# A MetaFormer layer on one core: reordered side work, and the first expert product packed by rows

## The chip, the cores and the metric

The kernel runs on one core of a Trainium2 chip. The metric is the device time of one execution in microseconds. The kernel before took 605.97 us in the median of three runs (603.32 to 607.88).

## The reference

The input x has 4 images of 96 channels and 56 x 56 pixels in fp32. The layer has two halves.

1. **Super-token attention.** Each pixel is normalised over its channels. The image is cut into 7 x 7 cells of 8 x 8 pixels; the mean of a cell is a super token. Each pixel has a softmax over the 9 super tokens around it (the affinities). Weighted sums of pixels give new super tokens, which go through attention with 8 heads of 12 (softmax over 49 tokens) and a projection; the result is spread back to the pixels by the affinities and added to x.
2. **A mixture of experts.** Each pixel is normalised again. A gate picks 2 of 4 experts. Each expert is `gelu(t @ w1 + b1) @ w2 + b2` with w1 96 x 384 and w2 384 x 96; the sum, weighted by the gate, is added to x. The kernel computes all four experts for each pixel, with weight 0 for those not picked.

```
h = gelu(einsum('bsd,edh->ebsh', x, w1) + b1)
y = einsum('ebsh,ehd->ebsd', h, w2) + b2
out = einsum('bse,ebsd->bsd', masked, y)
```

## The kernel before

An image is 28 tiles of 112 pixels. Four tiles are a **unit** of 448 pixels (the 8 rows of one row of cells). For each unit and each expert there is a **slot**: 28 slots an image, 112 in all. Everything else of an image is **side work**, done for image b+1 or b+2 between the slots of image b. All queues are written out by hand, with semaphores; nothing is planned by a program. TABLE names, for slot and half of slot, which side step PE does; READER names the engine that reads the step's bank. BEFORE is the order ahead of the first slot, the head.

**A slot.** `first_layer(i)` (L1121) makes z for 384 hidden values in three banks. The operands are split in fp16 high and low parts, so each third takes three products of 448 columns: w1_hi with the tokens' high part, w1_hi with their low part, w1_lo with the high part; 97 rows each, 96 channels and one of ones that brings in the bias. Two sets of three banks alternate. ACT reads z twice, GELU to fp16 (`hidden_high`, L469) and GELU to fp32 (`hidden_full`, L477). DVE takes the difference (`low_part`, L811). `second_layer(i)` puts the bias in with one product of 384 columns (L1130), then 24 products of 96 columns with the high part (L1136) and 12 with the low part (L1141), into one bank, Y. DVE adds the bank to xt in four instructions, weighted by the gate (`add_expert`, L824). PE's order in slot i is: side step, first_layer(i+2), side step, second_layer(i). The first layer waits for h_ready of slot i-2, the second for sum_done of slot i-1. DVE's order is: side read, low_part(i+1), side read, further side work, add_expert(i).

**Side work by kind.** SF (L962): sums of cells, read by DVE; CEN: centring, read by ACT; LOG (L978): affinity logits and gate logits, read by DVE; affinity_shift on DVE, exp on ACT, sums and scales on DVE and POOL; SFT (L989): the super sums over 28 tiles, in four parts; SUPT, QKV, SCO, PRT, HEA, HET, PRO: the attention, in small products; AFT: turned affinities; PIX (L1065): pixels out of super tokens, added by DVE; TRN (L1076): turned tokens for the first layer, copied by ACT (L436) to xhl.

**Deviations.** The first normalisation's 1/sqrt (`deviation_begin`, `deviation_end`) and the second's (`pixel_variance`, `pixel_deviation`) are chains of small DVE instructions with a wait after each: a shift trick for the start and three Newton steps of three instructions, on 112 x 28 values.

**Tables.** ACT uses Exp for the affinities (slot 2), for the attention (slot 9) and for the gate (slot 23), and GELU in each slot. Each change loads a table.

**Queues.** SP has the input transfers, one transfer of b2's low part, the channel loads (`load_channels`, 1.2 MB each), and one store a unit. ACT's queue has the constants and the weights at the start.

The names that the change touches:

Of the kernel before, what the change touches and what calls it, by code (L numbers as in the profile page):

```python
# [50 lines left out]
NORMAL = {0: 2, 3: 3, 8: 4, 13: 5, 17: 6}  # L51
# [6 lines left out]
def constants():  # L58
# [16 lines left out]
    ones = np.tile(np.concatenate([np.ones(IMG), np.zeros(IMG)]), 2)[None]  # L75
    return (table.astype(np.float32), row.astype(np.float32), cells.astype(np.float32), near.astype(np.float32),
            ones.astype(np.float16))


def build(nc, x, xtok, table, inner, cells, near, ones, wqkv, wproj, bproj, projx, gate_w, gate_b, w1, b1, w2, b2, out):  # L80

    with ExitStack() as ctx:
# [18 lines left out]
        scrap = sb("scrap", [1, 2])  # L101
        spare = sb("spare", [1, 1])
# [6 lines left out]
        w1_hi = sb("w1_hi", [CB, E * HID], F16)  # L109
        w1_lo = sb("w1_lo", [CB, E * HID], F16)  # L110
# [20 lines left out]
        seed = sb("seed", [PT, T], I32)  # L131
# [14 lines left out]
        prob = sb("prob", [128, 4, N])  # L146
        probT = sb("probT", [N, 4, 128])
# [6 lines left out]
        xhl = sb("xhl", [CB, 2, 2, IMG], F16)  # L154
# [13 lines left out]
        def own_super(r0, r1):  # L168
# [4 lines left out]
        w1_st = stage[0:CB, 0:E * HID]  # L173
# [8 lines left out]
            ones_in zeros_set pool_set ident16_set gatew_done gatew_set w_hi weights_set  # L182
            cell_ready shifted exp_ready scale_ready aff_ready affr_ready
            aff_hi aff_lo prob_ready so_hi so_mid norm_ready xs_ready xhi_ready xlo_ready
            gate_shifted gate_exp gate_ready
            side_done side_act side_dve z_done hh_ready h_ready hl_ready y_done sum_done
            norm1_step norm2_step attn_step gate_step weights_step""".split()
# [13 lines left out]
                  + [(0, "PIX", 0), (1, "SF", 0), (0, "PIX", 1), (1, "SF", 1), (0, "PIX", 2), (1, "SF", 2),  # L201
                     (0, "PIX", 3), (1, "SF", 3), (0, "PIX", 4), (0, "PIX", 5), (0, "PIX", 6), (1, "CEN", 0)]
                  + [(1, "LOG", k) for k in range(4)] + [(0, "TRN", 0)])
        BETWEEN = [(0, "TRN", 1)]

        TABLE = {(2, 0): (0, "TRN", 2), (5, 0): (0, "TRN", 3),
                 (6, 0): (1, "SFT", 0, 0, 4), (6, 1): (1, "SFT", 0, 1, 4), (7, 0): (1, "SFT", 0, 2, 4),
                 (7, 1): (1, "SFT", 0, 3, 4), (8, 0): (1, "SUPT", 0), (8, 1): (1, "QKV", 0), (9, 0): (1, "SCO", 0),
                 (9, 1): (1, "AFT", 0), (10, 0): (1, "AFT", 1), (10, 1): (0, "TRN", 4), (11, 0): (1, "PRT", 0),
                 (11, 1): (1, "HEA", 0), (12, 0): (1, "HET", 0), (12, 1): (1, "PRO", 0), (13, 0): (1, "PRO", 1),  # L210
                 (13, 1): (1, "AFT", 2), (14, 0): (1, "AFT", 3),
                 (15, 0): (1, "PIX", 0), (15, 1): (2, "SF", 0), (16, 0): (1, "PIX", 1), (16, 1): (2, "SF", 1),
                 (17, 0): (1, "PIX", 2), (17, 1): (0, "TRN", 5), (18, 0): (1, "PIX", 3), (18, 1): (2, "SF", 2),
                 (19, 0): (1, "PIX", 4), (19, 1): (2, "SF", 3), (20, 0): (1, "PIX", 5), (20, 1): (2, "CEN", 0),
                 (21, 0): (1, "PIX", 6), (21, 1): (0, "TRN", 6), (22, 0): (2, "LOG", 0), (22, 1): (2, "LOG", 1),
                 (23, 0): (2, "LOG", 2), (23, 1): (2, "LOG", 3), (25, 0): (1, "TRN", 0), (27, 0): (1, "TRN", 1)}
# [16 lines left out]
        visits += [(v, SIDE) for v in BETWEEN]  # L233
# [23 lines left out]
        def last_before_slots(bank):  # L257

            return [u for u, where in visits[0:len(BEFORE)] if where == bank][-1]
# [9 lines left out]
        def project_rows(k):  # L269
            return (range(0, 5), range(5, G))[k]  # L270

        @block.sync
        def _(sp):
# [17 lines left out]
            sp.dma_start(b2_hl[1:2, :], b2_low[:]).then_inc(S["b2_moved"], 16)  # L291
            for b in range(B):
                if b + 2 < B:
                    sp.wait_ge(S["side_done"], number[(b + 1, "LOG", 3)] + 1)
                    load_channels(b + 2)
                for r in range(G):
                    sp.wait_ge(S["sum_done"], b * SLOTS + (r + 1) * E)
                    sp.dma_start(out[b * IMG + r * UT:b * IMG + (r + 1) * UT, :].rearrange("(t p) c -> p t c", p=PT),
                                 rows_of(b, r)[:, :, 0:C]).then_inc(S["out_stored"], 16)
# [3 lines left out]
        def _(pool):  # L303
            for n, (what, value) in enumerate((
                    (ones16[:], 1.0), (aoT[:], 0.0), (vT[:], 1.0), (qm[:], 0.0), (gw[:], 0.0),
                    (hh[:, :, :, UT:FW], 0.0), (hl[:, :, :, UT:FW], 0.0), (aff16[:], 0.0))):
                pool.memset(what, value).then_inc(S["pool_set"], 1)
                pool.wait_ge(S["pool_set"], n + 1)
# [13 lines left out]
            def tokens_low(b, r):  # L322
# [3 lines left out]
                pool.tensor_tensor(x16[:, rows, 1, :], xs[:, rows, :], x16[:, rows, 0, :], ALU.subtract  # L326
                                   ).then_inc(S["xlo_ready"], 1)

            affinities_low(0)
            for r in range(2):  # L330
                tokens_low(0, r)
            for b in range(B):
                for slot in range(SLOTS):
                    if slot in NORMAL:
                        tokens_low(b, NORMAL[slot])
                    if b + 1 < B:
                        if slot == 4:
# [3 lines left out]
                        if slot in (23, 24):  # L341
                            tokens_low(b + 1, slot - 23)

        @block.scalar
        def _(act):
            for dst, src, name in (
# [3 lines left out]
                    (wqkv_sb[:], wqkv, "small_in"), (gate_bb[:], gate_b.to_broadcast([128, E]), "small_in"),  # L350
                    (xhl[C:CB, :, :, :].rearrange("p i h n -> p (i h n)"), ones, "ones_in")):
                act.dma_start(dst, src).then_inc(S[name], 16)
            act.wait_ge(S["zeros_set"], 1)
            act.activation(scrap[:, 1:2], scrap[:, 0:1], ACT.Exp)
            act.wait_ge(S["xch_in"], 16)
            for dst, src in ((w1_st[0:C, :], w1), (w1_st[C:CB, :], b1), (w2_st, w2), (b2_st[:], b2)):
# [6 lines left out]
            def split_weights():  # L363
                act.wait_ge(S["weights_in"], 64)
                act.activation(w1_hi[:], w1_st, ACT.Copy, scale=WS).then_inc(S["w_hi"], 1)
                act.activation(w2_hi[:].rearrange("p a c -> p (a c)"), w2_st, ACT.Copy, scale=WS
                               ).then_inc(S["w_hi"], 1)
                act.activation(b2_hl[0:1, :], b2_st[:], ACT.Copy, scale=WS).then_inc(S["w_hi"], 1)

# [32 lines left out]
            def attention_exponentials(b):  # L402
                act.wait_ge(S["side_dve"], reads_up_to((b, "SCO", 0)))
                act.activation(prob[:], prob[:], ACT.Exp, scale=float(HD) ** -0.5).then_inc(S["prob_ready"], 1)
# [19 lines left out]
            def tokens_high(b, r):  # L424
# [5 lines left out]
                act.copy(x16[:, rows, 0, :], xs[:, rows, :]).then_inc(S["xhi_ready"], 1)  # L430

            def tokens_turned(b, r):
                bank = opened((b, "TRN", r))
                if r == 0 and b >= 2:
                    act.wait_ge(S["z_done"], (b - 1) * SLOTS)
                act.copy(xhl[0:C, b % 2, :, r * UT:(r + 1) * UT],  # L436
                         bank[0:C, 0:UT].bitcast(F16).rearrange("p (h n) -> p h n", h=2)).then_inc(S["side_act"], 1)
# [33 lines left out]
            def hidden_full(i):  # L471
                z = ps[:, CH * (i % 2):CH * (i % 2) + CH, 0:UT]
                if i < 2:
                    act.wait_ge(S["weights_set"], 1)
# [5 lines left out]
            split_weights()  # L480
            affinity_exponentials(0, 0)
            affinity_exponentials(0, 1)
            affinities_high(0)
# [46 lines left out]
        def _(dve):  # L530
# [354 lines left out]
            for k in range(4):  # L885
                logits(1, k)
# [348 lines left out]
```

## Time and profile before

| | |
|---|---|
| Median of three runs | 605.97 us |
| Time of the profiled execution | 601.96 us |
| Its span | 600.1 us |
| PE busy | 548.2 us (91%) |
| DVE busy | 452.7 us (75%) |
| ACT busy | 378.9 us (63%) |
| POOL busy | 66.4 us (11%) |
| Mean granted TensorE clock | 0.92 of full speed |

Busy time is the time in which an engine has an instruction under way; matmuls are pipelined, so the mean length of one (358 ns for a product of 448 columns) is longer than its share of PE's time. The chain of waits gives the share: it goes back from the last instruction to what released each.

### The profile page before, as it was taken

The page shows a single profiled execution, that of the slowest core. Times are in us where ns is not written, and L with a number is a line of the kernel's source. Part 1 is how long each engine was busy: PE and PEld are TensorE (multiplying, and loading weights), DVE is VectorE, ACT ScalarE, POOL GpSimd, SP SyncE. Part 2 cuts the span into 40 slices and gives each one's busy share as a digit, 9 for nine tenths or more (in the row PEclk, how much of TensorE's full clock was granted, in tenths as well). Part 3 has the DMA queues.
Part 4 walks back from the last instruction along what each step waited for, and adds up shares of the span by engine and source line. Part 5 has one row for each costly group of instructions (what it writes and reads, how often), then busy time and mean ns, then how long its engine had stood idle before and what let it go on. Part 6 is the DMA issues. An engine that isn't in the chain of part 4 may idle for free.

```text
span 600.1 us, 15640 instructions
## 1 busy us (share of the span) xinstructions
PE 548.2 (91%) x6612; PEld 426.1 (71%) x6612; DVE 452.7 (75%) x1303; ACT 378.9 (63%) x387; POOL 66.4 (11%) x47
## 2 busy tenths in 40 slices
PE   8997768899889999989889999989899899999996
PEld 4995764667657877668658787768677676777774
DVE  6178645887597889978587889977479998778775
ACT  0035008865784658885783658884877777777773
POOL 3010000130010101140010101140001011111100
PEclk9559557989898989999898999999899989999999
DMA  9951003000000000300000000000000000000000
GB/s 213 236 135 36 2 1 80 14 2 13 14 2 13 14 2 14 93 14 13 8 7 13 14 2 14 13 14 13 1 14 13 14 14 14 13 14 14 13 14 24
DMA packets 15595, 17.49 MB, mean 29 GB/s; under 512 B 13781, under 2 KB 13917, under 8 KB 15134
## 3 DMA queue, kind: packets, MB, share of 16 engines
q1 hardware_dynamic: 14498, 14.76, 10.1%
q10 hardware_dynamic: 1028, 1.74, 1.2%
q8 instruction: 52, 0.85, 0.6%
q14 instruction: 17, 0.14, 0.1%
HBM read 11.68 MB, written 4.82 MB: 27 GB/s over the span
## 4 chain that ended last, share of the span: by engine, by line
PE 65%; DVE 13%; ACT 11%; issue 5%; DMA 5%; ACTq 0%; SPq 0%; DVEq 0%
PE ps L1121 24%; PE ps L1136 15%; PE ps L1141 7%; ACT hh L469 4%; PE ps L978 3%; PE ps L962 3%; DMA b_st<-b 3%; PE ps L1130 3%; ACT h L477 3%; PE ps L989 2%; DVE xt L824 2%; PE ps L1076 2%; DMA xch<-x 2%; DVE hl L811 2%; PE ps L1065 1%
## 5 line engine op out<-in xcount | busy, mean ns | idle before, releaser
L469 ACT ACTIVATE hh<-ps 128x1344 f16<-128x1344 f32 x112 | 144.7, 1292 | 84.0 <-PE ps L1121 82.9
L811 DVE TENSOR_TENSOR hl<-h,hh 128x1344 f16<-128x1344 f32 x112 | 175.6, 1568 | 20.4 <-ACT h L477 20.1
L1121 PE MATMUL ps<-xhl,w_hi 97*128 97x448 f16 x672 | 185.7, 358 | 1.1 <-ACT xhl L436 1.1
L824 DVE SCALAR_TENSOR_TENSOR xt<-ps,gl,xt 112x96 f32<-112x96 f32 x448 | 110.7, 309 | 65.9 <-PE ps L1141 65.6
L477 ACT ACTIVATE h<-ps 128x1344 f32<-128x1344 f32 x112 | 144.1, 1287 | 0.0
L1136 PE MATMUL ps<-w_hi,hh 128*128 128x96 f16 x1344 | 134.9, 211 | 0.0
L1136 PE MATMUL ps<-w_lo,hh 128*128 128x96 f16 x1344 | 134.9, 211 | 0.0
L1136 PEld LDWEIGHTS ps<-w_lo,hh 128*128 128x128 f16 x1344 | 121.2, 101 | 8.4 <-issue 1.3
L1136 PEld LDWEIGHTS ps<-w_hi,hh 128*128 128x128 f16 x1344 | 122.4, 101 | 4.8 <-issue 0.2
L1121 PE MATMUL ps<-xhl,w_lo 97*128 97x448 f16 x336 | 120.1, 357 | 0.0
L326 POOL TENSOR_TENSOR x<-xs,x 112x384 f16<-112x384 f32 x28 | 47.1, 1681 | 448.2 <-ACT x L430 448.2
L1121 PEld LDWEIGHTS ps<-xhl,w_hi 97*128 97x128 f16 x672 | 61.2, 100 | 45.4 <-issue 4.8
L1141 PE MATMUL ps<-w_hi,hl 128*128 128x96 f16 x1344 | 79.0, 211 | 0.0
L1141 PEld LDWEIGHTS ps<-w_hi,hl 128*128 128x128 f16 x1344 | 66.8, 101 | 0.0
L1121 PEld LDWEIGHTS ps<-xhl,w_lo 97*128 97x128 f16 x336 | 33.1, 99 | 32.2 <-issue 2.0
L436 ACT COPY xhl<-ps 96x896 f16<-96x896 f16 x28 | 25.3, 902 | 32.2 <-PE ps L1076 31.9
L1130 PE MATMUL ps<-b_hl,ones 128*128 128x384 f16 x112 | 38.3, 342 | 6.8 <-DVE xt L824 6.7
L978 PE MATMUL ps<-sfw,xch 103*112 103x31 f32 x224 | 33.5, 317 | 10.9 <-ACT sfw L373 9.4
L978 PEld LDWEIGHTS ps<-sfw,xch 103*112 103x112 f32 x224 | 32.9, 242 | 12.3 <-ACT sfw L373 8.9
L962 PEld LDWEIGHTS ps<-cellw,xt 112*96 112x96 f32 x224 | 27.5, 213 | 7.0 <-issue 5.5
L962 PE MATMUL ps<-cellw,xt 112*96 112x7 f32 x224 | 27.7, 260 | 4.8 <-DVE xt L701 3.9
L430 ACT CAST x<-xs 112x384 f16<-112x384 f32 x28 | 14.3, 512 | 26.1 <-DVE xs L730 26.1
(136 smaller groups left out, 482.2 us busy)
## 6 DMA issues: line engine op xcount, KB each, us to landing
xt<-xtok SPq DMA_DIRECT2D x8, 624.8 KB, 13.9
xch<-x SPq DMA_DIRECT2D x4, 1176.0 KB, 7.5
out<-xt SPq DMA_DIRECT2D x28, 168.0 KB, 2.3
h<-w ACTq DMA_DIRECT2D x2, 576.0 KB
wqkv_sb<-wqkv ACTq DMA_DIRECT2D x1, 228.0 KB
tab<-table ACTq DMA_DIRECT2D x1, 119.5 KB, 5.5
xch<-cells ACTq DMA_DIRECT2D x1, 85.8 KB
projx_sb<-projx ACTq DMA_DIRECT2D x1, 36.4 KB, 12.6
```

The costliest lines, as they stand in the source:

```text
L326: pool.tensor_tensor(x16[:, rows, 1, :], xs[:, rows, :], x16[:, rows, 0, :], ALU.subtract).then_inc(S["xlo_ready"], 1)
L436: act.copy(xhl[0:C, b % 2, :, r * UT:(r + 1) * UT], bank[0:C, 0:UT].bitcast(F16).rearrange("p (h n) -> p h n", h=2)).then_inc(S["side_act" ...
L469: act.activation(hh[:, i % 3, :, 0:UT], z, ACT.Gelu, scale=1.0 / WS).then_inc(S["hh_ready"], 1)
L477: act.activation(h32[:, i % 2, :, :], z, ACT.Gelu, scale=1.0 / WS).then_inc(S["h_ready"], 1)
L811: dve.tensor_tensor(hl[:, i % 2, :, 0:UT], h32[:, i % 2, :, :], hh[:, i % 3, :, 0:UT], ALU.subtract).then_inc(S["hl_ready"], 1)
L824: ins = dve.scalar_tensor_tensor(out=xt[:, b, t, 0:C], in0=ps[0:PT, Y, j * C:(j + 1) * C], scalar=gl[:, b % 2, t, e:e + 1], in1=xt[:, b, t ...
L962: ins = pe.matmul(o[0:C, c0:c0 + G], xt[:, b, t, 0:C], cellw[:, t, :], start=(j == 0), stop=(j == TU - 1))
L978: ins = pe.matmul(o[0:PT, (t - t0) * NLOG:(t - t0 + 1) * NLOG], xch[:, t * PT:(t + 1) * PT], sfw[:, t // TU, :], start=True, stop=True)
L1121: ins = pe.matmul(ps[:, CH * (i % 2) + c, 0:UT], ww[:, w0:w0 + 128], xhl[:, b % 2, half, r * UT:(r + 1) * UT], start=(n == 0), stop=(n == 2))
L1130: pe.matmul(y, ones16[:], b2_hl[:, e * C:(e + 1) * C].unsqueeze(1).to_broadcast([128, TU, C]), start=True, stop=False, skip_group_check=True)
L1136: pe.matmul(y[:, j, :], hh[:, i % 3, c, j * PT:j * PT + 128], ww[:, e * CH + c, :], start=False, stop=False, skip_group_check=True)
L1141: ins = pe.matmul(y[:, j, :], hl[:, i % 2, c, j * PT:j * PT + 128], w2_hi[:, e * CH + c, :], start=False, stop=(j == TU - 1 and c == CH - ...
```

## The change

- **Row packing.** x minus its mean has channels that add up to zero, so channel 95 of the normalised tokens is dropped: the last row of w1 is subtracted from the others (POOL, once), and its place is taken by ones and the bias. The three products of 96 rows are 288 rows: `w1_a` and `w1_b` are 128 rows each, and the last 32 rows, one third for each of the three hidden thirds, lie in three ranges of 32 partitions (`w1_c`), with the tokens copied there as well (`xhc`). So a slot has 6 products on 128 rows and 3 on 32 rows.
- **Copies.** For each unit, SP copies 64 partitions of 448 columns within xhl and twice 32 partitions to xhc (`spread`), behind ACT's evacuation, which is now two copies (128 and 64 partitions). The first layer waits for them. Six transfers put the weights in place in the head.
- **Deviations.** Except for image 0 both deviation chains run on POOL (`deviation` in slot 8, `pixel_deviation` in slot 21), in operations that POOL has: four instructions a Newton step in place of three, six for the variance.
- **Attention's softmax.** exp becomes (1 + tanh(z/2)) / (1 - tanh(z/2)): Tanh on ACT, three instructions on DVE (`attention_weights`).
- **Order.** The affinity logits, shifts and exponentials of image b+2 come at the end of image b; the affinity exponentials and the gate's are now together in slot 25. The attention steps come a slot earlier. The head has the logits of image 1 behind the first two first layers, the statistics of image 1 beside the cell sums of image 0, and the pixel statistics of image 0 ahead of the cell sums of image 1.

```diff
-NORMAL = {0: 2, 3: 3, 8: 4, 13: 5, 17: 6}
+NORMAL = {0: 2, 1: 3, 5: 4, 11: 5, 13: 6}
...
+            def spread(b, r):
+                sp.wait_ge(S["side_act"], reads_up_to((b, "TRN", r)))
+                cols = slice(r * UT, (r + 1) * UT)
+                sp.dma_start(xhl[2 * ZONE:128, b % 2, 1, cols], xhl[0:2 * ZONE, b % 2, 0, cols]
+                             ).then_inc(S[f"xhl_moved{r % 2}"], 16)
+                for k in range(2):
+                    sp.dma_start(xhc[k * ZONE:(k + 1) * ZONE, b % 2, cols], xhl[2 * ZONE:C, b % 2, 0, cols]
+                                 ).then_inc(S[f"xhl_moved{r % 2}"], 16)
...
+            def pixel_deviation(b):
+                pool.wait_ge(S["pixels_done"], b)
+                pool.wait_ge(S["xs_ready"], b * G)
+                pool.wait_ge(S["gate_shifted"], b)
+                ps1.mark(pool.tensor_tensor(momp[:, 4, :], st2[:, :, 1], st2[:, :, 4], ALU.add))
+                variance(ps1, st2, momp, 1e-5)
+                newton_begin(ps1, rstd2[:], momp[:, 3, :], seedp)
+                for _ in range(3):
+                    newton_step(ps1, rstd2[:], momp[:, 3, :], newtp)
+                ps1.link(pool.tensor_tensor(momp[:, 4, :], momp[:, 4, :], rstd2[:], ALU.mult))
+                pool.tensor_scalar(mr[:], momp[:, 4, :], -0.5, None, ALU.mult).then_inc(S["norm_ready"], 1)
...
-                act.activation(prob[:], prob[:], ACT.Exp, scale=float(HD) ** -0.5).then_inc(S["prob_ready"], 1)
+                act.activation(prob[:], prob[:], ACT.Tanh, scale=0.5 * float(HD) ** -0.5).then_inc(S["prob_tanh"], 1)
...
+            def attention_weights(b):
+                dve.wait_ge(S["prob_tanh"], b + 1)
+                at.link(dve.tensor_scalar(pden[:], prob[:], -1.0, 1.0, ALU.mult, ALU.add))
+                at.link(dve.reciprocal(pden[:], pden[:]))
+                dve.scalar_tensor_tensor(out=prob[:], in0=prob[:], scalar=1.0, in1=pden[:], op0=ALU.add, op1=ALU.mult
+                                         ).then_inc(S["prob_ready"], 1)
...
@@ first_layer
-                for c in range(CH):
-                    w0 = e * HID + c * 128
-                    for n, (ww, half) in enumerate(((w1_hi, 0), (w1_hi, 1), (w1_lo, 0))):
-                        ins = pe.matmul(ps[:, CH * (i % 2) + c, 0:UT], ww[:, w0:w0 + 128],
-                                        xhl[:, b % 2, half, r * UT:(r + 1) * UT], start=(n == 0), stop=(n == 2))
+                cols = slice(r * UT, (r + 1) * UT)
+                for part, ww in enumerate((w1_a, w1_b)):
+                    for c in range(CH):
+                        w0 = e * HID + c * 128
+                        ins = pe.matmul(ps[:, CH * (i % 2) + c, 0:UT], ww[:, w0:w0 + 128], xhl[:, b % 2, part, cols],
+                                        start=(part == 0), stop=False)
+                for c in range(CH):
+                    rows = slice(c * ZONE, (c + 1) * ZONE)
+                    third = xhc[rows, b % 2, cols] if c < 2 else xhl[rows, b % 2, 0, cols]
+                    ins = pe.matmul(ps[:, CH * (i % 2) + c, 0:UT], w1_c[rows, e, :], third, start=False, stop=True)
...
```

The further side steps in a slot on DVE, after the change (b the image of the slots): sums of affinities of b+1 in slots 2 and 3, weights in 4, statistics of b+2 in 4 to 7 (7 tiles each), attention weights in 9, pixel statistics of b+1 in 14 to 20, shifts of b+2 in 22 and 24, normalise of b+1 in 23 and 27, the gate's logits in 25, ranks in 26 and weights in 27. PE's: SFT in 5 and 6, SUPT and QKV in 7, SCO in 8, AFT in 9, PRT and HEA in 10, HET and PRO in 11, PIX in 14 to 20, SF of b+2 in 14 to 18, LOG of b+2 in 20 to 22, and TRN of unit 0 of b+1 in 24.

## Rows read from the trace of the kernel before

**Rows 1.** Windows cut by image: length, busy us of each engine (instructions), granted clock, DMA
```profile
0.00:105.62 105.62, 86.01 (x575) 70.87 (x575) 62.19 (x247) 28.90 (x44) 8.53 (x15) 0.69 0.41 100
105.62:243.75 138.13, 129.10 (x1631) 100.34 (x1632) 110.79 (x323) 94.11 (x96) 15.89 (x9) 0.95 0.05 13
243.75:380.16 136.41, 127.78 (x1634) 99.91 (x1633) 110.71 (x323) 94.47 (x96) 16.22 (x10) 0.96 0.07 17
380.16:504.03 123.87, 115.55 (x1520) 87.62 (x1519) 99.79 (x263) 94.10 (x93) 15.78 (x10) 0.97 0.05 12
504.03:600.10 96.07, 89.79 (x1258) 67.35 (x1256) 69.22 (x151) 67.38 (x59) 10.01 (x5) 1.00 0.06 14
```

**Rows 2.** Chain of waits, last image, one slot: start us, us, what
```profile
542.06 1.70 PE ps L1121 x9
543.76 0.16 PE ps L1130
543.93 1.02 PE ps L1136 x24
544.95 0.51 PE ps L1141 x12
```

**Rows 3.** Costliest groups on the page, DVE in every slot: busy us, mean ns
```profile
L811 DVE TENSOR_TENSOR hl<-h,hh 128x1344 f16<-128x1344 f32 x112 | 175.6, 1568 | 20.4 <-ACT h L477 20.1
L824 DVE SCALAR_TENSOR_TENSOR xt<-ps,gl,xt 112x96 f32<-112x96 f32 x448 | 110.7, 309 | 65.9 <-PE ps L1141 65.6
```

**Rows 4.** Chain of waits of a middle image, large side steps
```profile
263.54 1.26 PE ps L989 x14
...
321.96 1.28 PE ps L962 x16
...
346.19 1.56 PE ps L978 x16
```

**Rows 5.** Windows of 4 us of that image (PE, PEld, DVE, ACT, POOL, then clock)
```profile
256.00:260.00 4.00, 1.50 (x35) 1.38 (x32) 2.79 (x5) 3.88 (x4) 1.82 (x1) 1.00 0.09 22
...
316.00:320.00 4.00, 4.00 (x49) 3.83 (x49) 1.40 (x7) 0.00 (x0) 0.00 (x0) 0.58 0.00 0
```

**Rows 6.** Chain of waits of that image, a table load and cold products
```profile
251.11 1.28 ACT L380
...
317.06 1.92 PE ps L1136 x24
```

**Rows 7.** Chain of waits of that image, behind products on 49 rows
```profile
295.89 0.27 PE ps L1130
...
297.86 1.81 PE ps L1121 x9
```

**Rows 8.** Timeline of DVE: first and last of the pixel deviation's 18 instructions
```profile
351.39 0.20 DVE L712 TENSOR_TENSOR mom<-st 112x28 f32<-112x28 f32 x1
...
354.82 0.19 DVE L721 SCALAR_TENSOR_TENSOR mr<-mom,rstd 112x28 f32<-112x28 f32 x1
```

**Rows 9.** Groups by shape: DVE's reciprocal
```profile
L772 DVE RECIPROCAL gs<-gs 112x28 f32<-112x28 f32 x4 | 1.3, 327 | 0.1
```

**Rows 10.** POOL's low part: two of them in its timeline, then the page's group
```profile
79.41 0.91 POOL L326 TENSOR_TENSOR x<-xs,x 112x384 f16<-112x384 f32 x1 [35.28 <-ACT x L430]
...
243.75 2.45 POOL L326 TENSOR_TENSOR x<-xs,x 112x384 f16<-112x384 f32 x1 [12.51 <-ACT x L430]
...
L326 POOL TENSOR_TENSOR x<-xs,x 112x384 f16<-112x384 f32 x28 | 47.1, 1681 | 448.2 <-ACT x L430 448.2
```

**Rows 11.** DMA issues: count, KB each, median us from issue to landing
```profile
out<-xt SPq DMA_DIRECT2D x28, 168.0 KB, 2.3
```

**Rows 12.** Chain of waits of the head
```profile
62.34 2.49 PE ps L962 x16
...
77.67 1.06 DVE xs L730 x4
79.65 10.66 PE ps L978 x56
```

More of the change, by code:

```diff
@@ L74, in constants, with build @@
     near = np.tile(np.concatenate([near, np.zeros((G, E))], axis=1), (1, G))
[L75 to L80, printed above, removed]
+    return table.astype(np.float32), row.astype(np.float32), cells.astype(np.float32), near.astype(np.float32)
+def build(nc, x, xtok, table, inner, cells, near, wqkv, wproj, bproj, projx, gate_w, gate_b, w1, b1, w2, b2, out):
     with ExitStack() as ctx:
@@ L291, in _ @@
             sp.dma_start(b2_hl[1:2, :], b2_low[:]).then_inc(S["b2_moved"], 16)
-            for b in range(B):
[L293 to L299, printed above, removed]
+            sp.wait_ge(S["w_hi"], 3)
@@ new lines, in store @@
+            def store(b, r):
+                sp.wait_ge(S["sum_done"], b * SLOTS + (r + 1) * E)
+                sp.dma_start(out[b * IMG + r * UT:b * IMG + (r + 1) * UT, :].rearrange("(t p) c -> p t c", p=PT),
+                             rows_of(b, r)[:, :, 0:C]).then_inc(S["out_stored"], 16)
+            spread(0, 0)
+            sp.wait_ge(S["side_done"], number[(1, "LOG", 3)] + 1)
+            load_channels(2)
+            for b in range(B):
+                for slot in range(SLOTS):
+                    for half in range(2):
+                        if read_at(b, slot, half) and read_at(b, slot, half)[1] == "TRN":
+                            spread(read_at(b, slot, half)[0], read_at(b, slot, half)[2])
+                    if slot == 1 and b > 0:
+                        store(b - 1, G - 1)
+                    if slot % E == 1 and slot > 1:
+                        store(b, slot // E - 1)
+                    if slot == 23 and b + 3 < B:
+                        sp.wait_ge(S["side_done"], number[(b + 2, "LOG", 3)] + 1)
+                        load_channels(b + 3)
@@ L1072, in turn_tokens @@
                 o = bank((b, "TRN", r))
[L1073 to L1077 removed]
+                for j in range(TU):
+                    both = x16[:, r * TU + j, :, :].rearrange("p h c -> p (h c)")
+                    for part, rows in enumerate((both[:, 0:128], both[:, 128:2 * C])):
+                        c0 = (part * UT + j * PT) // 2
+                        ins = pe.transpose(o[0:rows.shape[1], c0:c0 + PT // 2].bitcast(F16), rows, ident16[0:PT, 0:PT])
                 ins.then_inc(S["side_done"], 1)
```

390 lines of the change are left out of this document (212 added, 178 removed).

## The prediction, made before the result was known

> **What bounds the kernel now.** I read the windows cut by image first, then the chain of waits of the last image, then the costliest groups, then the chain and 4 us windows of a middle image, and last the head.
>
> The third normalisation of each image on POOL marks the images: 105.62, 243.75, 380.16 and 504.03 us, so the head takes 105.6 us and the images 138.1, 136.4, 123.9 and 96.1 [rows 1]. PE is busy for 93 to 94% of each, DVE for 80% of the first three. In the last image the chain is PE alone: nine products 1.70, bias 0.16, 24 products 1.02 and 12 more 0.51, which is 3.40 us a slot [rows 2]. DVE needs in a slot 1.57 for the low part and 4 x 0.25 = 0.99 for the add [rows 3]; started back to back the two take 2.45. So a bare slot is PE's, with 0.95 us of room on DVE.
>
> The side work fills that room unevenly. In a full image PE has 28 x 3.40 = 95.2 of slots and 25 of side work at full clock: 4 x 1.26 for the super sums, 3.5 x 1.28 for the cells, 3.5 x 1.56 for the logits [rows 4], and 10 for the small steps of the same view. That makes 120. The images take 16 to 18 more. Where it goes: the exponentials of the next image load a table (1.28) ahead of the GELU and another behind it, and PE is busy 1.50 of 4 us [rows 5, 6]; and after DVE's deviation chains PE falls to its lower clock (granted 0.58 in 316 to 320), where the 24 products take 1.92 in place of 1.02 [rows 5, 6].
>
> **Part 1, the first layer.** Six full passes stay: 6 x 1.70 / 9 = 1.13. Three products of 32 rows follow. The trace has no such product, so bounds: side by side they take the time of one, 0.19; one after another 0.57. The three write three banks and read three ranges of partitions, so nothing in the code orders them: I take 0.19. But PE must change its tile there and back. After eight products on 49 rows the bias takes 0.27 in place of 0.16, and behind a single 49-row turn the nine products take 1.81 in place of 1.70 [rows 2, 7]: 0.10 for each change. So 1.13 + 0.10 + 0.19 + 0.10 = 1.53 (1.32 to 1.90), 0.17 less than now in each slot, and up to 0.2 more than now at the bad end. The Trainium skill, TensorEngine Tiling (Array Packing), Key Properties, says that changing the tiling mode drains the engine, while different tiles may run in parallel; by the second half alone the layer would take 1.32, by both it is my 1.53, and the 0.10 steps agree with the first.
>
> **Part 2, vector work.** Both deviation chains of an image go to POOL: the second is 18 instructions from 351.39 to 355.01, 3.6 us [rows 8], the first about as long: 7 less. Added on DVE: three operations on 196 columns for the attention weights. Reciprocal on 28 columns takes 0.33, against 0.18 for a plain one of that size [rows 8, 9]; at the 5 to 6 ns a column that the difference gives, plus 1 ns as in every operation, 196 columns cost 1.4, and the other two 0.36 each: 2.1. DVE is 5 us lighter an image, at 105 of busy time.
>
> I put the new slots side by side, PE at 3.23 + side work, DVE at 2.45 + its extra work, and took the larger of each. Examples: slots 5 and 6 (half of the super sums each) 5.7; slots 14 to 16 (pixels and cells) 4.7; slot 21 (logits) 5.9; slot 27 (normalise and gate weights) 5.15 by DVE; slot 9 (attention weights) 4.45 by DVE. The 28 sum to 121.7, and to 111.6 for image 2, which prepares no image beyond the next. The same sum for the slots of before gives 126.7 against the 137 measured, so 10 are waits that the table does not see. Of these the tables and the cold clock behind them are the larger part and go: exp is now loaded once an image, with the gate's, and tanh should need no load beside GELU (no trace shows it; with its own load as now, 2.6 more on ACT an image). I keep 4. Images 0 and 1: 126 each; image 2: 115.6. **Image 3** has PE work alone: 26 x 0.17 = 4.4 less, 91.6. DVE's add has to fit under a first layer that is shorter: add 0.99, two hand-overs of about 0.2, against 1.53, so it still does.
>
> The Trainium skill, ScalarE: Activation LUTs, Table sets, names tanh in the sets of exp and sigmoid and not in GELU's; by that the two loads of the attention stay, some 8 us over three images, inside my range.
>
> **Part 3, the copies.** Each of the 28 units now waits for three SP transfers before its first layer. A store lands in 2.3 us [rows 11]. The nearest turn is one and a half slots ahead of its use, 5 us, and the turn, an evacuation of about 1 and 2.3 fit in about 4: nothing, while SP is free. SP's queue has stores and one channel load before them; each waits for something a slot old. If the cover fails, 2.3 us a unit. The weights' transfers (six, one after the DVE split at about 55 us) land long before the first layer. The extra row of weights to 95 partitions delays the weights by about 3 us, but the first exponentials no longer wait behind them.
>
> **Part 4, POOL.** A deviation is now 23 (pixels) or 25 operations in a chain. POOL's 112x384 takes 0.91 alone and 2.45 when DVE's low part runs [rows 10]. Bounds for one of 28 columns: 0.2, as on DVE, to 2.45. I take 0.3 and a lock-out of 4.6 for three low parts: 11.5 us, in a window of about 12 between the last statistics (slot 20) and normalise (slot 23). I charge 1.5 an image, 4.5.
>
> **Part 5, the head.** The pixel statistics of image 0 no longer alternate with PE's cold cell sums (2.49 for 16 products [rows 12]) and end some 5 us sooner; the deviation (22 steps of 0.2, 4.4 us) then runs beside the sums, 3.5 x 2.7 from about 63.5, and waits for their last at 73. Normalise moves from 77.67 [rows 12] to about 74. The logits of image 1 (10.66 us at the lower clock [rows 12]) move behind the first two layers, which have warmed PE up: about 6. Against that: the transfer 2.3, two table loads 2.6 [rows 6], shifts (about 2) taken into the head. The mark at 105.62 moves to 99.
>
> **Sum.** 99 + 126 + 126 + 115.6 + 91.6 + 4.5 = 562.7 of span, against 600.1; outside it 1.9 (601.96 was that run's time): 564.6. The median of the runs, 605.97, lies 0.7% above the profiled one, so 568 on its scale; I say 566.
>
> **Rivals.** *More gain*: the change of tile is hidden by the loads, the layer takes 1.33, and fewer waits stay (2): 118.3 + 2 twice, 108.8 + 2, 96.1 - 26 x 0.37 = 86.5, head 99: 537 to 541, some 543 on the median's scale. For it: weight loads run ahead now; against it: the 0.10 steps. 0.20.
> *No overlap*: three passes one by one and two changes, 1.90: images 133.3, 133.3, 122.7, 101.3, head 99, 4.5: 594 of span, 600 on the scale. Nothing in the trace excludes it. 0.08.
> *DVE becomes the bound*: the table's PE and DVE differ by under 0.5 us in half the slots; POOL's 48 operations more an image hold DVE up as its low part holds POOL up now [rows 10], at an eighth of a microsecond each 6 us an image: 584. 0.13.
> *SP late*: the channel load of image 3 and the late stores hold up the copies: half of the 28 units at 2.3, 32 us: 596. 0.04.
> *Slower*: POOL's pixel chain. 23 steps at 1.68, the mean of its 384-column step [rows 10], are 38.6 us, 26.6 over the window, three times: 80 more than the forecast, less the 4.5 charged: 640. DVE stands in normalise, the add and the second layer behind it. It decides from where 3 x (23x - 12) eats the 40 gained, x = 1.1 us a step. For it: 2.45 has been seen; against it: memsets of this size are short, and 384 columns alone took 0.91. 0.05.
>
> **Chances.** Forecast 0.50 (550 to 584), rivals as above. A measurement here can tell about 1%, 6 us, from no change. Faster: 0.50 + 0.20 + 0.13 + 0.03 + 0.04 = 0.90; same 0.05 (half of no overlap); slower 0.05. The range runs from 543 (more gain) to 590, leaving out half of the first rival's lower side, no overlap and slower.
>
> **What would show it.** The nine products' piece in the last image becomes 1.53, with the three products' starts apart by far less than 0.19; a bare slot 3.23. Two table loads an image in place of six. The granted clock stays at the upper level in slots 12 to 16 (0.58 now). POOL's chain of 23 ends within 12 us, and DVE's normalise of slot 23 does not wait. It would be wrong if the third pass costs 0.57, if DVE idles in slot 23, or if PE waits for a copy at a unit's first layer.

## The result, and the profile after

The changed kernel takes 609.06 us (median of 20 runs, 604.21 to 613.45); the kernel before took 604.82 us beside it. The ratio is 1.0064, 95% interval 1.0038 to 1.0089: slower by 0.6%, which is less than the 1% that the prediction called the least a measurement here can tell, where 566 us was forecast. The profiled execution has a span of 605.2 us.

The windows of the changed kernel, cut by image at the same mark as [rows 1], the third low part of an image's tokens on POOL (length, busy us of PE, PE's weight loads, DVE, ACT and POOL, then granted clock and DMA):

```profile
0.00:106.74 106.74, 87.82 (x569) 69.59 (x570) 64.19 (x240) 29.32 (x48) 18.82 (x43) 0.67 0.44 112
106.74:243.43 136.69, 128.81 (x1634) 94.01 (x1633) 106.86 (x289) 92.25 (x103) 30.95 (x58) 0.96 0.10 24
243.43:380.05 136.62, 128.73 (x1634) 94.04 (x1633) 106.26 (x288) 89.12 (x99) 31.13 (x58) 0.96 0.07 17
380.05:508.94 128.89, 118.64 (x1523) 83.73 (x1521) 97.32 (x246) 88.08 (x94) 23.92 (x32) 0.96 0.07 17
508.94:605.20 96.26, 90.00 (x1259) 62.57 (x1258) 69.39 (x151) 67.68 (x64) 10.70 (x5) 1.00 0.09 22
```

Against the forecast of 99, 127.5, 127.5, 117.1 and 91.6 (with 1.5 of POOL's charge in each of the middle three) that is 7.7, 9.2, 9.1, 11.8 and 4.7 us too much, 42.5 in all. DVE is lighter by 3.9, 4.5 and 2.5 us in the middle three, where 5 was forecast, and PE's busy time has not fallen but risen, from 548.2 to 554.0 us. Yet the chain of waits of the last image shows the bare slot just as it was worked out, 3.23 us where it was 3.40 [rows 2]:

```profile
541.27 1.13 PE ps L1209 x6
542.40 0.30 PE ps L1214 x3
542.70 0.27 PE ps L1222
542.97 1.02 PE ps L1228 x24
543.99 0.51 PE ps L1233 x12
```

What is dearer is a step that the prediction never priced. L1163 turns (transposes) a unit's tokens: eight turns, now alternately 128 and 64 columns wide. Groups of PE by shape in the changed kernel, and behind them the one of the kernel before, whose eight turns are all 96 wide:

```profile
L1163 PE MATMUL ps<-ident,x 112*64 112x112 f16 x112 | 28.1, 250 | 0.0
L1163 PE MATMUL ps<-ident,x 112*128 112x112 f16 x112 | 25.8, 231 | 20.2 <-issue 18.2 <-ACT affT L511 1.6 <-DVE xt L800 0.3
```

```profile
L1076 PE MATMUL ps<-ident,x 112*96 112x112 f16 x224 | 16.4, 218 | 15.3 <-issue 8.9 <-ACT affT L394 6.4
```

In the chain of waits of the kernel before such a group takes 0.40 us:

```profile
344.10 0.40 PE ps L1076 x8
```

In the chain of the changed kernel the group takes 1.19 us, and the first layer's six products behind it 1.24 in place of 1.13:

```profile
514.78 1.19 PE ps L1163 x8
515.97 1.24 PE ps L1209 x6
```

The second sign is "issue 18.2": PE stood 7 times at the turns, and the profile names nobody who released it. By the code the turn waits for the float16 halves of the tokens, the last of which is POOL's low part. Cut by stretches, the waits lie in two places at each change of image: at the first unit's turn in slot 24 (2.0, 2.0 and 4.8 us) and at the second unit's in slot 0 (2.6, 2.6 and 1.9); the seventh, 2.3, is in the head. The chain of the second place, where the second unit is normalised in slot 27 (DVE L832), then copied, split and turned, with PE at its lower clock behind it (granted 0.50 in the last window below; the 24 products take 1.92). The first window holds the stall at the first unit's turn:

```profile
371.61 1.05 DVE xs L832 x4
...
372.69 0.52 ACT x L547
...
374.35 1.81 PE ps L1163 x8
376.15 0.43 PE ps L1222
376.59 1.92 PE ps L1228 x24
```

```profile
351.00:355.00 4.00, 2.15 (x26) 1.14 (x23) 3.96 (x11) 1.83 (x3) 2.02 (x1) 1.00 0.00 0
371.00:375.00 4.00, 1.42 (x10) 0.49 (x8) 3.83 (x12) 1.98 (x3) 0.91 (x1) 0.89 0.01 2
375.00:379.00 4.00, 4.00 (x40) 3.31 (x40) 3.29 (x9) 2.81 (x4) 0.00 (x0) 0.50 0.06 15
```

The cold stretch of before behind DVE's deviations [rows 5] is gone: from 303 to 351 us the granted clock is 1.00 and PE is busy 47.95 of 48. But the new order has stalls of its own, a little later in the image.

### The profile page after: what moved, and what is told of

It is laid out like the page before. It is cut to its first block, busy times and chain, and to the rows that moved or that the text cites. A ratio compares the mean times of both kernels' runs of the same rounds, so it can differ in the third digit from the quotient of the medians.

```text
span 605.2 us, 15823 instructions
## 1 busy us (share of the span) xinstructions
PE 554.0 (92%) x6612; PEld 403.9 (67%) x6612; DVE 444.0 (73%) x1208; ACT 366.5 (61%) x407; POOL 115.5 (19%) x194
## 4 chain that ended last, share of the span: by engine, by line
PE 69%; DVE 10%; ACT 9%; issue 8%; POOL 2%; DMA 2%; SPq 0%; DVEq 0%; ACTq 0%
PE ps L1209 17%; PE ps L1228 14%; PE ps L1233 7%; PE ps L1163 6%; PE ps L1063 5%; PE ps L1047 5%; PE ps L1214 4%; PE ps L1222 3%; ACT h L598 3%; PE ps L1074 3%; ACT hh L590 2%; DVE xt L924 1%; DMA xt<-xtok 1%; DVE xs L832 1%; DVE pden L776 1%
## 5 line engine op out<-in xcount | busy, mean ns | idle before, releaser
L402 POOL TENSOR_TENSOR x<-xs,x 112x380 f16<-112x380 f32 x28 | 41.3, 1476 | 302.6 <-ACT x L547 302.6
L1209 PE MATMUL ps<-xhl,w_a 128*128 128x448 f16 x336 | 87.1, 370 | 4.7 <-DMA xhc<-xhl 4.2
L1209 PE MATMUL ps<-xhl,w_b 128*128 128x448 f16 x336 | 84.5, 361 | 0.0
L1163 PE MATMUL ps<-ident,x 112*128 112x112 f16 x224 | 40.4, 240 | 20.2 <-issue 18.2
L1209 PEld LDWEIGHTS ps<-xhl,w_b 128*128 128x128 f16 x336 | 33.9, 101 | 33.9 <-issue 5.3
L557 ACT COPY xhl<-ps 128x448 f16<-128x448 f16 x28 | 14.9, 533 | 65.8 <-PE ps L1163 65.8
L1163 PEld LDWEIGHTS ps<-ident,x 112*128 112x128 f16 x224 | 23.3, 104 | 38.7 <-issue 24.8
L1214 PE MATMUL ps<-xhc,w_c 32*128 32x448 f16 x224 | 40.8, 361 | 0.0
L1214 PE MATMUL ps<-xhl,w_c 32*128 32x448 f16 x112 | 40.4, 361 | 0.0
L1209 PEld LDWEIGHTS ps<-xhl,w_a 128*128 128x128 f16 x336 | 28.1, 102 | 18.3 <-issue 7.2
```

The source lines that it names most:

```text
L402: pool.tensor_tensor(x16[:, rows, 1, 0:C - 1], xs[:, rows, 0:C - 1], x16[:, rows, 0, 0:C - 1], ALU.subtract).then_inc(S["xlo_ready"], 1)
L1163: ins = pe.transpose(o[0:rows.shape[1], c0:c0 + PT // 2].bitcast(F16), rows, ident16[0:PT, 0:PT])
L1209: ins = pe.matmul(ps[:, CH * (i % 2) + c, 0:UT], ww[:, w0:w0 + 128], xhl[:, b % 2, part, cols], start=(part == 0), stop=False)
L1214: ins = pe.matmul(ps[:, CH * (i % 2) + c, 0:UT], w1_c[rows, e, :], third, start=False, stop=True)
```

## The experiments

Thirteen kernels ran besides the changed one. Medians are in us; the ratio is to the kernel before on the same chip. Where two kernels were not measured beside each other, their ratios compare better than their medians. Windows and chains are of one execution each. "Full" is the changed kernel with turns of one size.

| kernel | median | ratio, 95% interval |
|---|---|---|
| changed kernel | 609.06 | 1.0064 [1.0038, 1.0089] |
| turns grouped by width | 594.62 | 0.9849 [0.9808, 0.9890] |
| turns of one size ("full") | 585.72 | 0.9693 [0.9644, 0.9742] |
| nine products, no packing | 596.54 | 0.9880 [0.9843, 0.9917] |
| one row group | 643.68 | 1.0670 [1.0621, 1.0719] |
| full, ScalarE reads late | 602.94 | 0.9977 [0.9943, 1.0011] |
| full, second unit early | 570.69 | 0.9419 [0.9372, 0.9466] |
| full, both | 584.83 | 0.9653 [0.9604, 0.9702] |
| full, exponential | 589.63 | 0.9736 [0.9689, 0.9784] |
| nine products, second unit early | 572.65 | 0.9502 [0.9437, 0.9567] |
| full, early, head's subtraction on DVE | 570.16 | 0.9445 [0.9403, 0.9488] |
| full, early, deviations on DVE | 589.17 | 0.9756 [0.9703, 0.9808] |
| full, early, logits first | 565.53 | 0.9345 [0.9317, 0.9373] |
| nine products, early, logits first | 574.02 | 0.9492 [0.9468, 0.9516] |

### The turned tokens

Theory A: each change of width costs PE about 0.10 us. Rival: these turns are slow whatever their order.

```diff
-for j in range(TU):
-    for part, rows in enumerate((both[:, 0:128], both[:, 128:2 * C])):
+for part in range(2):
+    for j in range(TU):
+        rows = (both[:, 0:128], both[:, 128:2 * C])[part]
```

> The eight turns of a tile row (4 of 128 columns, 4 of 64, alternating in the changed kernel) are put in the order 4 of 128, then 4 of 64; nothing else is changed. Theory A (each change between a 128-column and a 64-column turn costs TensorE about 0.10 us, as any change of the tile does): the group of eight falls from 1.18 to 1.30 us to 0.5 to 0.65, 28 groups give back 0.6 each where TensorE is the bound: about 592 us (609 minus 17). Theory B (the turns are slow in themselves, by their 128 weight columns and float16 reads, whatever their order): the group stays at 1.2 us and the time at 609.

```diff
-x16 = sb("x16", [PT, T, 2, C], F16)
+x16 = sb("x16", [PT, G, TU * 2 * C + 64], F16)
...
-for part, rows in enumerate((both[:, 0:128], both[:, 128:2 * C])):
+for part, rows in enumerate((both[:, 0:128], both[:, 128:256])):
```

> The second turn of each tile reads 128 columns too (the 64 behind its own are the next tile's or padding, and nobody reads what they become), so that all eight turns of a tile row have one tile size, the one of the matmuls around them. Theory A (tile changes cost): the group falls to 0.40 to 0.50 us and the first layer behind it from 1.24 to 1.13; 28 times 0.85 is 24 us, less where another engine holds the slot: 586 to 590 us. Theory B (128-column turns are dearer by themselves): 1.2 us or more for the group and 609 or more for the kernel.

Measured 594.62 and 585.72. The chain of each kernel, around one turn of the last image; grouped first, then one size:

```profile
540.14 0.62 PE ps L1164 x8
540.76 0.27 PE ps L1223
```

```profile
534.46 0.50 PE ps L1167 x8
534.96 0.16 PE ps L1226
```

The group takes 1.19 alternating (seven changes inside), 0.62 grouped (one inside, one ahead, as it stands behind the 32-row products) and 0.50 in one size (one ahead). With 0.40 for the eight turns themselves (the value of the nine-product kernel below) each change costs 0.11: (1.19 - 0.40) / 7, 0.22 / 2, 0.10 / 1. The bias behind turns of one size needs no change either and is back at 0.16. Eight changes less in each of 28 units are 25 us by this; the ratios differ by 0.037, 22.5 us. Theory A holds; the rival falls, since both experiments turn 128 columns too, the second nothing else. The split between the two was off: grouping gave 13 us where six changes less are 18. The kernel with one row group below, whose turns alternate too, agrees: there the group stands behind 32-row products, with eight changes, and takes 1.29 us.

### Packing alone, and the row groups

> The change without its packing: new order, deviations on GpSimd, tanh, the constant channel, but the first layer is nine products of 96 rows as before, eight turns of 96 columns, one copy of both halves and no spreading transfers. Theory A (the packing gains 0.17 a slot, 19 us over 112 slots, and its turns and waits give back 24 or more): 600 to 606 us, turn group 0.40, bare slot 3.40. Rival (packing is a gain, the new order is the loss): slower than the changed kernel, 620 to 628 us.

```diff
-for part, ww in enumerate((w1_a, w1_b)):
-    ...
-    third = xhc[rows, b % 2, cols] if c < 2 else xhl[rows, b % 2, 0, cols]
-    ins = pe.matmul(..., w1_c[rows, e, :], third, start=False, stop=True)
+for n, (ww, part) in enumerate(((w1_a, 0), (w1_a, 1), (w1_b, 0))):
+    ...
+    ins = pe.matmul(..., ww[0:C, w0:w0 + 128], xhl[0:C, b % 2, part, cols], start=(n == 0), stop=(n == 2))
```

Measured 596.54, below the 600 to 606 expected and far from the rival's 620. So everything in the change but the packing is a gain of 1.2% by itself, and the packing as it was made cost 0.018 of the ratio, 11 us. Its chain in the last image:

```profile
539.18 1.71 PE ps L1190 x9
540.88 0.40 PE ps L1145 x8
541.28 0.16 PE ps L1199
```

> The three 32-row products of the first layer all read rows 64 to 95 (for two of the three with the third's weights), so they can't run beside each other. If the three row groups of the changed kernel do run side by side (0.30 us for the three), the third pass now takes 3 times 0.19 plus 0.10, 0.67 us: the bare slot goes from 3.23 to 3.60 and the kernel to 640 to 650 us. If they ran one after another already, nothing changes: 609.

In this kernel two of the three products use rows and weights that are not their own, so what it computes is not the layer; only its time is of use.

```diff
-rows = slice(c * ZONE, (c + 1) * ZONE)
+rows = slice(2 * ZONE, C)
```

Measured 643.68. The chain of its last image:

```profile
573.35 0.67 PE ps L1213 x3
```

0.67 against 0.30 is what the three row groups save by running side by side, in each of 112 slots: 41 us by the sum, 35 measured. The three products' records in the changed kernel start within 0.01 us of each other; this run shows that the gain is real and not a way of recording.

### What the turn waits for

Four kernels on the full one.

```diff
-for half in range(2):
-    if read_at(b, slot, half):
-        side_read(read_at(b, slot, half))
+if read_at(b, slot, 0):
+    side_read(read_at(b, slot, 0))
 if i + 2 < ALL:
     hidden_high(i + 2)
     hidden_full(i + 2)
+if read_at(b, slot, 1):
+    side_read(read_at(b, slot, 1))
```

> Base: the kernel with eight turns of one size (585.72 us). ScalarE reads a second side step of a slot behind the two activations of that slot and not before them. Theory (ScalarE stands at the turned tokens while the first layer it would work on has long been done; 22 such waits, 50.8 us in all, some on the path): the waits on the turns shrink and the kernel gains 1 to 1.3 us at each of the 4 or 5 such steps of images 0 to 2 that end a slot: 573 to 581 us. Rival (those waits have slack, and the copies now come later, with the spreading transfers behind them): 584 to 588.

It fell, and by much: 602.94, 17 us more than the full kernel. All side steps of the slots share one bank of PSUM, so the next one on PE waits until ScalarE has read the last. PE's waits for ScalarE's reads of the turned tokens, which the full kernel does not have, are 11.4 us here (9 times). In its chain the GELUs now stand ahead of the read, and PE's next turn (L1089) behind it:

```profile
277.55 1.29 ACT hh L594
278.84 1.18 ACT h L602
280.02 0.42 ACT xhl L561
280.44 0.42 ACT xhl L562
280.87 0.14 issue
281.00 0.56 PE ps L1089 x8
```

ScalarE's 50.8 us of waits on the turned tokens were slack; the early place in its queue was the right one.

```diff
-if slot == 23:
-    normalise(b + 1, 0)
+if slot in (23, 24):
+    normalise(b + 1, slot - 23)
...
-(0, 1): (0, "TRN", 1), ... (24, 1): (1, "TRN", 0)
+(25, 0): (1, "TRN", 0), (27, 0): (1, "TRN", 1)
```

> Base as before. The next image's second tile row is normalised in slot 24 and not in slot 27, its float16 halves are made right behind, its turn goes from slot 0 of the next image to slot 27, and the first row's turn from the second half of slot 24 to the start of slot 25. Theory (TensorE stands at these two turns, 17.1 us over 7 waits, and its clock falls behind them): 2 to 4 us for each of the three changes of image, 574 to 580 us. Rival (the turn of an image is set by the gate's chain on VectorE and the tables on ScalarE, and the waits only move): 583 to 588.

Measured 570.69, 15 us less than the full kernel, more than the 6 to 12 expected. The windows of its four images:

```profile
110.09:236.54 126.45, 118.90 (x1638) 88.58 (x1636) 107.61 (x289) 92.23 (x103) 29.61 (x57) 1.00 0.14 33
236.54:361.39 124.85, 118.33 (x1635) 88.40 (x1632) 107.60 (x288) 88.95 (x99) 31.80 (x57) 1.00 0.07 18
361.39:477.96 116.57, 107.76 (x1521) 77.91 (x1518) 97.79 (x244) 87.92 (x94) 27.62 (x32) 1.00 0.08 19
477.96:570.00 92.04, 85.45 (x1258) 60.47 (x1255) 69.62 (x151) 67.38 (x64) 10.93 (x5) 1.00 0.09 21
```

The first three are 5.0, 5.1 and 5.9 us shorter than in the full kernel (131.41, 129.90, 122.51). PE's wait at the turned tokens fell from 17.1 us to 3.1, and the granted clock is 1.00 in every image, where it was 0.99, 0.97 and 0.98 in the first three of the full kernel. These 14.0 us of waits are by themselves more than the estimate. Behind the old stalls the 24 products took 1.92; PE's busy time in the three images fell by 5.6 us, but part of that is paid back in other waits. The edit moves both turns, the second unit's chain to an earlier slot and the first unit's turn to a later one. In the full kernel the first unit's turn had 2.0, 2.0 and 4.8 us of the waits and the second unit's 1.7, 2.6 and 1.6, so both matter; no run separates them.

Both diffs together:

> Both edits together. If both theories hold and the waits are separate, the gains add: 565 to 575 us. If they are the same waits seen twice, the time is that of the better of the two alone.

Measured 584.83, outside the 565 to 575 expected from two gains. The edits are nearly additive (by the ratios 0.0284 lost, 0.0274 gained, 0.0040 gained together), but the first is a loss: 14 us more than the second alone.

```diff
-act.activation(prob[:], prob[:], ACT.Tanh, scale=0.5 * float(HD) ** -0.5)
+act.activation(prob[:], prob[:], ACT.Exp, scale=float(HD) ** -0.5)
...
-at.link(dve.tensor_scalar(pden[:], prob[:], -1.0, 1.0, ALU.mult, ALU.add))
-at.link(dve.reciprocal(pden[:], pden[:]))
-dve.scalar_tensor_tensor(out=prob[:], in0=prob[:], scalar=1.0, in1=pden[:], ...)
```

> Base as before, but attention takes the exponential itself and VectorE's three operations behind the tanh (0.23 + 1.39 + 0.48 us) go; ScalarE then has to load its table of exponentials and the one of Gelu again, 1.28 us each, three times. Theory (the two chains weigh about the same, 2.1 against 2.6, and the loads hold Gelu up too): 586 to 590 us. Rival (the tanh's chain on VectorE is what the slots wait for): 579 to 583.

Here the exponential is taken directly, with 18 table loads in place of 12. Measured 589.63, 0.4% over the full kernel, with intervals that overlap: the direction is as expected, the size is not settled. The tanh is at worst no loss.

### Who carries the deviations, and the head

```diff
-ps1 = Steps(pool, "deviation_step")
+ps1 = Steps(dve, "deviation_step")
...
+if slot == 21:
+    pixel_deviation(b + 1)
+if b + 2 < B and slot == 8:
+    deviation(b + 2)
```

> Base as before. Both chains of deviations (some 25 and 23 dependent operations of 28 columns) run on VectorE, in one piece each at slots 8 and 21, and no longer on GpSimd. Theory (a chain of about 5 us in front of VectorE's own work of a slot holds the low parts and the sums up, twice an image; on GpSimd it holds nobody): 3 to 5 us for each of the five chains in the slots, 582 to 595 us. Rival (VectorE's small operations take 0.2 us and the ones on GpSimd up to 1.6, so that the normalisation is ready 4 us sooner and VectorE has the room): 565 to 573.

Measured 589.17, 18.5 us more than the median of its base (20 by the ratios); the images are 7.1, 5.5 and 2.3 us longer. The rival falls. In this order POOL is the right place, slow as single operations there are.

```diff
-pool.tensor_tensor(w1_st[0:C - 1, :], w1_st[0:C - 1, :], w1_last, ALU.subtract)
...
+dve.tensor_tensor(w1_st[0:C - 1, :], w1_st[0:C - 1, :], w1_last, ALU.subtract)
 split_weights((1, 2))
```

> Base: the kernel of 570.69 us. The subtraction on the first layer's weights in the head (3.42 us on GpSimd) goes to VectorE, behind the affinities. Theory (while GpSimd runs it, VectorE's product of 432 columns takes 3.78 us where it took 0.61 before, and it stands on the head's path): the product falls to about 0.6, the head is 3 us shorter: 566 to 569 us. Rival (the head waits for the weights' halves and their transfers anyway): 570 to 572.

No difference: 570.16 against 570.69. That POOL holds DVE up is real. In the timeline of the base, POOL's subtraction and the DVE product that ran into it, and below it the same product in the changed kernel, where it started before the subtraction:

```profile
37.48 3.42 POOL L443 TENSOR_TENSOR h<-h,xs 95x1536 f32<-95x1536 f32 x1 [3.23 <-DMA xs<-w]
...
37.59 3.78 DVE L738 TENSOR_TENSOR affr<-aff,affs 112x432 f32<-112x432 f32 x1
```

```profile
36.99 0.61 DVE L734 TENSOR_TENSOR affr<-aff,affs 112x432 f32<-112x432 f32 x1
```

With the subtraction on DVE the product takes 0.61 again. But then the head's chain goes through ScalarE's split, which waits for the weights to land at 36.86 us. The theory of a 3 us gain fell.

The next kernel joins two diffs shown above, the nine products and the second unit early.

> The kernel with nine products of 96 rows (no packing, 596.54 us), with the next image's second tile row normalised and turned early as in the run of 570.69 us. The two differ from here on by the packing alone. Theory (bare slot 3.40 against 3.23, 0.17 in 112 slots less 0.10 in each of 28 turns and what other engines hold: 12 to 16 us): 582 to 587 us. Rival (with the stalls gone, VectorE and ScalarE set most slots and the packing has nothing to give in them): 572 to 578 us.

Measured 572.65, in the rival's range. The packing seemed worth 2 us by the medians and 5 by the ratios (0.9502 and 0.9419, with intervals that overlap), where the windows behind the head show 9.8 for it (469.7 us in all unpacked, 459.9 packed). The rest was looked for in the head. In the packed kernel PE waits once for 5.0 us on the spreading transfers, with its clock still low; the rows are the waits of the kernel with the second unit early, and its head's chain:

```profile
PE ps L1212 <- DMA xhc<-xhl: 5.0, 1, 5.0
```

```profile
88.19 1.84 DMA xhc<-xhl
...
90.17 2.40 PE ps L1212 x6
...
95.44 8.12 PE ps L1066 x56
```

Its 56 logits products take 8.12 us; in the unpacked kernel they take 5.44. That price is not paid each time: in the changed kernel they take 5.64 behind a wait of 4.2. The last pair puts two of the four logits pieces into that wait:

```diff
+for v in BETWEEN[0:2]:
+    side(v)
 first_layer(0)
 ...
 first_layer(1)
-for v in BETWEEN:
+for v in BETWEEN[2:]:
     side(v)
```

> Base: the kernel of 570.69 us. In the head TensorE does two of the next image's four pieces of logits before the first two first layers and not behind them. Theory (the packed first layer waits 5.0 us for its spreading transfers with TensorE idle, and TensorE's clock is still at 0.58 in the stretch behind; the logits fill this wait): the wait goes, 3 to 5 us: 565.5 to 568 us. Rival (the first hidden layer comes as much later as the logits take, and ScalarE and VectorE, idle in the head, wait for it): 570 to 573.

> The same order of the head with nine products of 96 rows and no transfers (572.65 us without it). Theory (there is no transfer to hide here, so only the order of the head changes): 572 to 575 us, and the packing alone is then worth the difference of the two, 6 to 8 us: the 10 us that its stretches behind the head show, less the clock's part of the head. Rival (the packing is worth 2 us, as the runs of 570.69 and 572.65 say): both orders gain or lose alike and stay 2 us apart.

Measured 565.53 and 574.02. The packed kernel gains 0.0074 of the ratio, 4.5 us, with intervals that just touch; the unpacked one gains nothing that can be told (0.9502 and 0.9492). The spans of the two packed profiles differ by more, 570.0 and 560.6, but of that 5.7 lie ahead of the edit, where the normalisation of the head begins at 81.53 us in one and at 75.83 in the other with the same instructions: heads are not compared from single executions. With the wait covered the packing is worth 0.0147, 8.9 us, clear of the intervals, and the best kernel is 6.5% faster than before. Its chain in the head has no transfer in it:

```profile
79.47 5.93 PE ps L1066 x32
85.41 2.24 PE ps L1212 x6
87.64 0.49 PE ps L1217 x2
88.14 2.30 PE ps L1212 x6
```

## Why the prediction was wrong

Three steps failed: the changes of tile in the turned tokens, put at nothing (22.5 us by the experiment); "I keep 4" for waits, which left out the turns at the change of image (16.6 us by the ratios); and the transfer in the head, priced at 2.3 where PE waits 4.2 to 5.0 (4.5 us by the ratios). Putting these right brings the kernel to 0.9345, which is 566.3 on the scale of the 605.97 shown, where the forecast was 566. That the two agree within 1 us is in part luck: the mended kernel has another order of turns and of the head than the one that was forecast, the forecast itself was rounded from 568 to 566 without a reason, and single terms in it are off: the packing gives 8.9 us in the end, where 0.17 in 112 slots is 19, and the head's normalise comes 4.5 us later than it was put.

**Part 1 held for the slot and failed for the turns.** "There and back", 0.10 each, 0.19 for three products side by side: 1.13 + 0.30 + 0.11, and the slot of 3.23 was measured to the hundredth. This is the first failure: the same rule was not applied to the turned tokens, which the packing makes 128 and 64 columns wide in alternation. Eight changes a unit, 28 units: 22.5 us by the experiment, more than the 19 that 0.17 in 112 slots can give. The prediction even counts "a single 49-row turn" as a change, and its rule from the Trainium skill, TensorEngine Tiling (Array Packing), Key Properties, says that changing the tiling mode drains the engine, and it makes no exception for columns; the trace agrees with it, at 0.11 us a change. Part 3 named "the turn" as a copy's source and never opened it.

**Part 2: "I keep 4" was the second failure.** With the turns mended the first three windows are still 131.4, 129.9 and 122.5, 3.9, 2.4 and 5.4 over the forecast, and more than that sat in two places that the table of slots cannot see: the chains of normalise, copy, low part and turn of the next image's first two units. One begins in slot 23 and its turn stood in slot 24, the other begins in slot 27 and is used in the next image's slot 0. The table charged slot 27 with 5.15 of DVE work and stopped there, though every term it added was the head of a chain across four engines. With the first turn later and the second chain earlier this gives 16.6 us by the ratios (0.9693 to 0.9419). With both mended the windows are 126.5, 124.9, 116.6 and 92.0 against a forecast of 126, 126, 115.6 and 91.6 (127.5, 127.5 and 117.1 with POOL's share): for this order the sum by slots comes out within 3 us an image. DVE lighter by 5: 4 measured.

**The rival of DVE as the bound** was partly true. By the slot's terms (28 x 0.17 less 7 x 0.10 for the turns) the packing gives about 4 us to each image; in the last pair of runs it gives 2.1, 2.3, 0.4 and 3.9. Only in the last image, bare of other work, is the whole of it seen. PE's wait for DVE's add is 13.5 us in the packed kernel of that pair and 10.4 in the unpacked one. So of the 19 us that 0.17 makes in 112 slots less than half reached the time, 8.9.

**Part 3 held in the slots, not in the head.** A copy lands in 1.9 us and in the changed kernel none is waited for later. In the kernels of 570.69 and 565.53, whose turns are moved, PE stands 0.7 to 1.4 us at a first layer at each change of image, which fits the copy by its time but has no releaser in the profile. In the head the forecast charged 2.3; the wait was 4.2 us in the changed kernel, and PE went through it at its lower clock. Covering it gave 4.5 us of the 7.7 that the head was too long. The remaining 3 or so lie ahead of it: the cell sums of image 1 begin at 68.01 us, where about 63.5 was forecast, and normalise at 78.54, where it was 74.

```profile
68.01 9.11 PE ps L1047 x56
78.54 1.04 DVE xs L832 x4
```

What makes them late is not shown and stays open.

**Part 4 held for two images of three.** The pixel chain on POOL runs from 337.75 to 347.64 us in the second, 9.9 for the 11.5 forecast, operations of 28 columns taking 0.21 to 0.28 and, when a low part of DVE is in the way, 1.58 to 1.68. In the third image it begins at 468.76, behind DVE's last statistics at 468.45, meets three low parts and ends at 479.91, and DVE's normalise waits for it, against the sign that the prediction named. PE's stall at the first turn there is 4.8 us and not 2.0:

```profile
DVE xs L832 <- POOL mr L434: 2.7, 1, 2.7
```

That lies inside the 4.5 charged. The rival that ended slower by this chain did not happen; the kernel lost its gain by another road, which was given no chance of its own. By the prediction's own 1% the outcome is "same", which it gave 0.05.

**The tables.** The prediction took tanh to need no load beside GELU, against the Trainium skill, ScalarE: Activation LUTs, Table sets, whose list names tanh in other sets. The trace is with the prediction: 12 loads in all for 22 before, and none between the tanh (L521) and the GELU behind it:

```profile
282.33 0.36 ACT L521 ACTIVATE prob<-prob 128x196 f32<-128x196 f32 x1
282.58 0.90 ACT L511 COPY affT<-ps 96x896 f16<-96x896 f16 x1
284.23 0.90 ACT L511 COPY affT<-ps 96x896 f16<-96x896 f16 x1 [0.75 <-PE ps L1084]
285.03 1.29 ACT L590 ACTIVATE hh<-ps 128x1344 f16<-128x1344 f32 x1
```

**"No overlap"** is shown false by the run with one row group: 0.67 there, 0.30 in the change.

## What to carry to other kernels

When a change alters the shape of an operand, price every instruction that touches it, the small helpers too: the matmuls gained 0.17 us each slot and the transposes that feed them lost more. Keep instructions of one tile size together on PE, and pad a narrow one to its neighbours' width where the extra columns are free. A table of slots finds what a slot costs, not what a chain across engines costs that starts in one of its last slots; for each value used at the start of the next stage, follow the chain of engines behind it, start it early enough and put its reader late enough.

## What the runs showed of the hardware

A change of tile size costs PE 0.11 us, between 128 and 64 columns as between 128 and 32 rows. Three products of 32 rows in three row groups take 0.30 us with the change, against 0.67 in one row group. A two-input operation on POOL (3.42 us) held a DVE operation for nearly its whole length, 3.78 us for one of 0.61; with the POOL operation gone it took 0.61. The other way round, operations of 28 columns on POOL take 0.21 to 0.28 us, and 1.58 to 1.68 beside DVE's low part. A short idle stretch of PE is paid for behind it too: at the change of image 24 products behind the stall at the second unit's turn took 1.92 in place of 1.02. Net of the waits that came in their place, taking away 14.0 us of stalls was worth 5.0, 5.1 and 5.9 us in the three images.
